# Attention features and two norms moved to ScalarE, the attention norm's scale and bias folded into the projections, and a new order of work in a three-stage pipeline

## The chip, the cores and the metric

The kernel runs on one core of a Trainium2 chip. The metric is the device time of one execution in microseconds (us), from launch to end. The profile is one execution recorded by the hardware profiler; its span is the time from the first to the last instruction. Five engines run side by side, each through its own queue in program order, and meet only at semaphores: TensorE (PE, with its weight loads PEld), VectorE (DVE), ScalarE (ACT), GpSimd (POOL) and SyncE (SP, which issues most DMAs).

## What is computed

Four layers, each a residual on a normed input, over `x` of 4 x 1024 x 256 float32. Cut to what matters:

```python
x = x + mamba(norm(x))          # projection, convolution, a scan over 1024 tokens, gate, projection, layer norm
x = x + ffn(norm(x))            # 8 experts 256 -> 256 -> 256, the two best weighted per token
x = x + attn_b(norm(x))
x = x + ffn(norm(x))            # the same weights as before

def attn_b(inputs):             # 16 heads of 16, causal linear attention
    x = layer_norm(inputs, ln1_scale, ln1_bias)
    q, k, v = x @ wq, x @ wk, x @ wv
    phi_q, phi_k = relu(q) + 0.001, relu(k) + 0.001
    num = phi_q . cumsum(phi_k v^T);  den = phi_q . cumsum(phi_k)
    x = (num / den) @ wo + inputs
    y = layer_norm(x, ln2_scale, ln2_bias)
    return x + gelu(y @ w1 + b1) @ w2 + b2
```

The scan is `s = clip(s * A + b_t x_t, -10, 10)` with a state of 256 x 32 per batch row, one token after another. It can't be reordered.

## The kernel before

`front_part` does the first projection, the convolution and the scan's operands for all tokens (some 95 us). `main_part` then goes over the 1024 tokens in 16 chunks of 64 tokens (4 batch rows x 64 = 256 rows, two tiles of 128). It is a pipeline of three stages that is written out by hand: `step(i, c, late)` scans chunk `i`, finishes the Mamba layer and runs the first expert layer and the attention of chunk `c = i - 1`, and runs the MLP's rest and the second expert layer of chunk `late = i - 2`. Step 1 has no `late`; then come 14 steps with all three stages (a hardware loop), then one without a scan and one with `late` alone. Each engine's function lists its operations in the order in which they go into its queue, so this list is the schedule.

- DVE: `scan(a, b)` makes scan steps a to b-1, each two multiplications (L1626) and two saturating additions (L1635), with ScalarE's `u(s)` (L928) as input, at most 8 ahead. Between them stand the norms' statistics (`ln_stats`), `add_expert` (L1748), `low_half`, `routing`, `mask`, `attended`, and, before the change, `ln_apply` for the outer norm (L1669), `ln_affine` for attention's norm (L1692, L1697), `key_feature` (L1820) and `query_feature` twice (L1826).
- PE: `y(n)` reads 8 finished scan steps (L1220). `first_layer` (L1287, three products of split operands, 12 matmuls) and `second_layer` (L1300, 4 matmuls) are an expert's two halves, `mlp_first` and `mlp_second` the MLP's. `tpose_set` transposes (L1234). The attention is `features` (L1375), `values` (L1382), `turn_k` (L1397), `scores` (L1408), `from_states` (L1418), `from_chunk` (L1428), `new_states` (L1439), `attention_out` (L1389).
- ACT: `relu` (L1035), `gelu` (L1055), `ln_apply` (L983), copies out of PSUM (`copy_set` L992, `copy_y` L1011, `copy_v`, `copy_k`), `spread_kv` (L1027).
- POOL: `rstd_of` makes a norm's factor in small steps (L821 to L828); `add_attention` (L879), `add_mlp_bias` (L872), `next_cblk` (L840).

PSUM has eight banks, and most are shared: `features` writes keys, then queries, into `HB[1]`, so the queries wait until `key_feature` has read the keys, and `TB` serves every transposition. `relu` of an expert stands between its `first_layer` and its `second_layer`, `add_expert` between one `second_layer` and the next on the same bank.

## Time and profile before

| | us |
|---|---|
| median of 3 runs | 1843.38 (1839.24 to 1846.09) |
| the profiled execution, its own time | 1845.13 |
| its span | 1843.3 |
| PE busy / DVE busy / ACT busy / POOL busy | 1693.8 / 1565.0 / 926.0 / 245.1 |
| from the start of step 1 to the start of step 2 | 104.8 |
| the 14 steps with all three stages | 1427.1, or 101.9 each |
| the two steps without a scan | 150.9 |

A step is counted here from one `gate_y` (L1760, four DVE instructions) to the next. Busy time is the union of an engine's instructions; an engine's idle time matters only where another waits for it.

### The profile page before, as it was taken

Reading aid. Unit: us, or ns where it says so; the run is one execution under the profiler, and the core shown is the slowest. Engines: PE = TensorE matmul, PEld = TensorE weight load, DVE = VectorE, ACT = ScalarE, POOL = GpSimd, SP = SyncE. Lnnn points to the kernel's source line nnn. Section 1 sums busy time; section 2 is a strip of 40 time slices with the busy share of each in tenths; the row PEclk is TensorE's granted clock in tenths of the full one; section 3 lists DMA queues with packets and bytes.
Section 4 is the critical chain, followed back from the end, with each engine's and each line's share of the span. In section 5 each row is a group of like instructions: output and inputs, shape, how many; then the busy total and the mean of one; then the engine's idle time right before and its main releaser. Section 6 shows DMA issues by size and latency. Waiting matters only on the chain. (4 is left out here: it accounts for less than half of the span.)

```text
span 1843.3 us, 55933 instructions
## 1 busy us (share of the span) xinstructions
PE 1693.8 (92%) x16992; PEld 1422.4 (77%) x16992; DVE 1565.0 (85%) x5957; ACT 926.0 (50%) x2134; POOL 245.1 (13%) x515
## 2 busy tenths in 40 slices
PE   5774889999999999999999999999999999999987
PEld 3332668787887878787888878787878878787986
DVE  6589879899998989898999999898989999997522
ACT  4674445463645555554645555455536455554322
POOL 1011011111102011110102020111101020111000
PEclk9886879999999989998999999899989999999998
DMA  6885333242333333332433323332423333330000
GB/s 191 298 247 147 110 94 99 77 117 75 102 96 90 100 84 110 91 96 77 110 87 93 107 81 98 100 99 81 117 71 93 105 89 104 93 98 20 1 7 6
DMA packets 108425, 182.63 MB, mean 99 GB/s; under 512 B 45288, under 2 KB 71936, under 8 KB 107648
## 3 DMA queue, kind: packets, MB, share of 16 engines
q1 hardware_dynamic: 107232, 178.71, 33.9%
q8 instruction: 146, 2.39, 0.6%
q14 instruction: 119, 0.97, 0.2%
q10 hardware_dynamic: 928, 0.56, 0.1%
HBM read 161.35 MB, written 17.83 MB: 97 GB/s over the span
## 5 line engine op out<-in xcount | busy, mean ns | idle before, releaser
L1635 DVE CUSTOM_DVE_ANT_0 state<-decayed_state,u_ring 128x128 f32<-128x128 f32 x2048 | 522.3, 293 | 11.1 <-ACT u_ring L928 4.7
L1626 DVE TENSOR_TENSOR decayed_state<-state,decay 128x128 f32<-128x128 f32 x2048 | 508.1, 289 | 2.7 <-POOL m_rstd L813 1.2
L1300 PE MATMUL bank<-f_w_sb,hs_whole 128*128 128x256 f32 x2048 | 488.3, 382 | 0.6 <-DVE res L1748 0.6
L928 ACT ACTIVATE u_ring<-xrep,b_steps 128x256 f32<-128x256 f32 x1024 | 450.5, 503 | 52.5 <-DVE state L1635 46.0
L1300 PEld LDWEIGHTS bank<-f_w_sb,hs_whole 128*128 128x128 f32 x2048 | 374.2, 191 | 45.9 <-DVE res L1748 1.0
L1035 ACT ACTIVATE hs_whole<-bank,f_b_sb 128x256 f32<-128x256 f32 x512 | 214.1, 470 | 373.1 <-PE bank L1287 373.1
L1287 PE MATMUL bank<-late_fT_parts,f_w_hi 128*128 128x256 f32 x1024 | 187.6, 306 | 0.0
L1287 PE MATMUL bank<-fT_parts,f_w_hi 128*128 128x256 f32 x1024 | 179.5, 297 | 4.6 <-DVE fT_parts L1678 3.4
L1220 PE MATMUL bank<-state,cblk 128*32 128x256 f32 x2048 | 151.3, 423 | 16.4 <-DVE state L1635 16.4
L1287 PEld LDWEIGHTS bank<-fT_parts,f_w_hi 128*128 128x128 f32 x1024 | 142.5, 189 | 23.3 <-DVE fT_parts L1678 7.1
L1287 PEld LDWEIGHTS bank<-late_fT_parts,f_w_hi 128*128 128x128 f32 x1024 | 149.8, 194 | 11.8 <-issue 5.8
L1748 DVE SCALAR_TENSOR_TENSOR x<-bank,comb,x 128x256 f32<-128x256 f32 x256 | 111.6, 478 | 19.5 <-PE bank L1300 19.4
L1748 DVE SCALAR_TENSOR_TENSOR res<-bank,comb,res 128x256 f32<-128x256 f32 x256 | 111.7, 478 | 15.5 <-PE bank L1300 11.7
L1300 PE MATMUL bank<-m_w_sb,hs_whole 128*128 128x256 f32 x512 | 118.3, 379 | 0.0
L1220 PEld LDWEIGHTS bank<-state,cblk 128*32 128x32 f32 x2048 | 59.2, 117 | 75.4 <-issue 36.3
L1300 PEld LDWEIGHTS bank<-m_w_sb,hs_whole 128*128 128x128 f32 x512 | 94.9, 190 | 11.6
L879 POOL TENSOR_TENSOR mb<-mb,a_t 128x512 f32<-128x512 f32 x16 | 20.5, 1279 | 608.2 <-DVE a_t L1813 608.2
L992 ACT ACTIVATE turn<-bank 128x512 f32<-128x512 f32 x48 | 28.6, 595 | 136.5 <-PE bank L1234 136.5
L821 POOL TENSOR_TENSOR m_ve<-m_mv,m_eps 128x2 f32<-128x2 f32 x96 | 20.7, 216 | 562.7 <-DVE m_mv L1662 562.7
L1287 PE MATMUL bank<-late_fT_parts,m_w_hi 128*128 128x256 f32 x512 | 91.4, 301 | 0.0
L1287 PE MATMUL bank<-late_fT_parts,f_w_lo 128*128 128x256 f32 x512 | 83.1, 286 | 0.0
L1287 PE MATMUL bank<-fT_parts,f_w_lo 128*128 128x256 f32 x512 | 81.0, 281 | 0.0
(157 smaller groups left out, 2296.3 us busy)
## 6 DMA issues: line engine op xcount, KB each, us to landing
xrep<-xs_dram SPq DMA_DIRECT2D x1024, 128.0 KB, 2.6
xt<-in_x SPq DMA_DIRECT2D x4, 1024.0 KB, 7.7
xn_dram<-xn SPq DMA_DIRECT2D x4, 1024.0 KB, 5.6
xs_dram<-xs SPq DMA_DIRECT2D x8, 512.0 KB, 4.4
f_w_sb<-in_f_w SPq DMA_DIRECT2D x2, 2048.0 KB
z_dram<-zT SPq DMA_DIRECT2D x8, 512.0 KB, 4.5
z_t<-z_dram SPq DMA_DIRECT2D x64, 64.0 KB, 2.3
out<-x SPq DMA_DIRECT2D x64, 64.0 KB, 2.1
```

What stands on the lines that cost most here:

```text
L821: pool.tensor_tensor(ve[:, k], mv[:, k, :, 1], eps[:, k], ALU.add).then_inc(ve_done[k].sem, 1)
L879: pool.tensor_tensor(mb[:], mb[:], a_t[:], ALU.add).then_inc(mb_done.sem, 1)
L928: act.activation(u_ring[:, s % USLOTS], xrep[:, slot, n], ACT.Copy, scale=b_steps[:, s // BSTEPS, s % BSTEPS:s % BSTEPS + 1]).then_inc(u_m ...
L992: act.activation(whole[:].rearrange("p k q -> p (k q)"), (HB[1] if k == T_WO else TB)[:], ACT.Copy).then_inc(tcopied[k].sem, 1)
L1035: act.activation(hs_whole[:, e % 2, m], hidden_bank(c, f, e)[:, m * TOK:(m + 1) * TOK], ACT.Relu, bias=g["f_b1"][:, e, m:m + 1]).then_inc( ...
L1220: last = pe.matmul(Y[YCOLS * j:YCOLS * (j + 1), tile * D:(tile + 1) * D], cblk[:, slot * YCOLS:(slot + 1) * YCOLS], state[:, s % RING, :], ...
L1287: last = pe.matmul(dst(tile), *((w_, d_) if stationary == "w" else (d_, w_)), start=first and stationary != "more", stop=(n == len(PRODUCT ...
L1300: last = pe.matmul(bank_[:, tile * D:(tile + 1) * D], hs_whole[:, slot, m, tile * P:(tile + 1) * P], w(m), start=(m == 0 and tile == 0 and ...
L1626: dve.tensor_tensor(decayed_state[:, part], state[:, (s - 1) % RING, part], decay[:, part], ALU.mult).then_inc(decayed.sem, 1)
L1635: dve._custom_dve(add_sat, out=state[:, s % RING, part], in0=decayed_state[:, part], in1=u_ring[:, s % USLOTS, part], s0=LIMIT, s1=-LIMIT) ...
L1748: dve.scalar_tensor_tensor(out=dst[:, tile], in0=out_bank(c, f, e)[:, tile * D:(tile + 1) * D], scalar=comb[:, f, tile, e:e + 1], in1=dst[ ...
```

## The change

1. The outer norm of attention's input moves from DVE (`ln_apply`, two instructions) to ScalarE (two `ln_apply` instructions, with a shift that POOL makes).
2. Attention's norm loses its scale and bias: ScalarE multiplies `wq`, `wk`, `wv` by `ln1_scale` once, in chunk 0, and PE makes the biases once. In the chunks ScalarE writes (x - mean) * rstd in two instructions, where DVE had four. The bias is added where the projections are read: in the features, and for the values in the copy before `attention_out` (two instructions for one).
3. The features move to ScalarE: `relu(x + bias)` per group of 128 rows, then `+ 0.001` over both groups; three instructions for one of DVE, three times per chunk.
4. POOL makes two small products more for each of the two norms. `add_attention` goes to the end of its queue.
5. The lists of all four engines are written in a new order.

```diff
+            def projections_scale(k):
+                act.wait_ge(mlp_bias_made.sem, 1)
+                for w in ("wq", "wk", "wv"):
+                    act.activation(g[w][:, k, :], g[w][:, k, :], ACT.Copy, scale=g["ln1_s"][:, k:k + 1]).then_inc(proj_scaled.sem, 1)
...
+                if k == T_WO:
+                    act.wait_ge(proj_bias_set.sem, 3)
+                    for kk in range(KD):
+                        act.activation(turn[:, kk], HB[1][:, kk * TOK:(kk + 1) * TOK], ACT.Identity,
+                                       bias=proj_bias[:, WV, kk:kk + 1]).then_inc(tcopied[k].sem, 1)
+                    return
...
+            def key_feature(c):
+                if c is None:
+                    return
+                act.wait_ge(proj_bias_set.sem, 3)
+                act.wait_ge(k_made.sem, k_made.after(c, 1))
+                for gr in range(KGROUPS):
+                    act.activation(kT[:, gr], HB[1][:, gr * TOK:(gr + 1) * TOK], ACT.Relu, bias=proj_bias[:, WK, gr:gr + 1]).then_inc(k_raw.sem, 1)
+                act.wait_ge(k_raw.sem, k_raw.after(c, KGROUPS))
+                act.activation(kT[:].rearrange("p k q -> p (k q)"), kT[:].rearrange("p k q -> p (k q)"), ACT.Identity,
+                               bias=g["feature_eps"][:, PADH // DH:PADH // DH + 1]).then_inc(kT_done.sem, 1)
+
+            def query_feature(c, half):
...
+                    act.activation(qT[:, KGROUPS * half + gr], HB[1][:, gr * TOK:(gr + 1) * TOK], ACT.Relu,
+                                   bias=q_bias[:, half, gr:gr + 1], scale=g["feature_own"][:, half:half + 1]).then_inc(q_raw.sem, 1)
```

Of ScalarE's list, from the outer norm to the scores:

```diff
+                ln_apply(c, OUTER, res, a_t, a_done)
                 u(33)
-                relu(late, 1, 0)
+                relu(late, 1, 2)
                 u(34)
                 u(35)
                 u(36)
+                ln_apply(c, LN1, a_t, turn, xl_done)
                 u(37)
...
                 u(43)
+                key_feature(c)
                 u(44)
+                u(45)
                 relu(late, 1, 4)
...
                 u(48)
+                query_feature(c, 0)
                 u(49)
+                copy_v(c)
+                query_feature(c, 1)
+                copy_k(c)
+                relu(late, 1, 5)
```

Of PE's list, the expert layers, then attention and the end of a step:

```diff
                 second_layer(c, 0, 3)
+                turn_comb(late, 1)
+                second_layer(c, 0, 4)
                 first_layer(c, 0, 5)
-                second_layer(c, 0, 4)
-                turn_comb(late, 1)
+                first_layer(c, 0, 6)
                 second_layer(c, 0, 5)
-                first_layer(c, 0, 6)
                 bias(late, 1)
+                second_layer(c, 0, 6)
                 first_layer(c, 0, 7)
...
                 features(g["wk"], k_made)
+                second_layer(late, 1, 3)
+                pe.wait_ge(kT_done.sem, kT_done.after(c, 1))
+                features(g["wq"], q_made)
+                values()
                 second_layer(late, 1, 4)
                 first_layer(late, 1, 5)
-                values()
-                pe.wait_ge(kT_done.sem, kT_done.after(c, 1))
-                features(g["wq"], q_made)
...
                 from_chunk(1).then_inc(num_made.sem, 1)
+                second_layer(late, 1, 6)
+                tpose_set(c, T_WO, at_done, HB[1])
+                y(5)
+                pe.wait_ge(tcopied[T_WO].sem, tcopied[T_WO].after(c, KD))
+                attention_out()
+                first_layer(late, 1, 7)
                 new_states(0).then_inc(kv_half.sem, 1)
                 wait_apart(kv_half, kv_half.after(c, 1))
                 new_states(1).then_inc(kv_made.sem, 1)
...
-                y(6)
+                second_layer(late, 1, 7)
                 pe.wait_ge(kv_added.sem, kv_added.after(c, 1))
                 tpose_set(c, T_MLP, yl_done)
-                second_layer(late, 1, 7)
-                y(OCTS - 1)
+                y(6)
...
                 mlp_first(c, 0)
+                y(OCTS - 1)
```

Of DVE's list, attention and the end of a step:

```diff
-                scan(43, 44)
-                query_feature(0)
-                query_feature(1)
-                scan(44, 46)
+                scan(47, 50)
                 mask(0)
...
-                scan(51, 57)
-                add_states()
-                scan(57, 59)
+                scan(55, 56)
+                add_expert(late, 1, 6, x3)
+                scan(56, 58)
                 add_attention()
                 ln_stats(c, LN2, a_t, xr_done, (1, 1))
-                scan(59, 61)
-                add_expert(late, 1, 6, x3)
-                scan(61, 64)
+                scan(58, 59)
+                add_states()
+                scan(59, 63)
                 low_half_mlp()
+                scan(63, 64)
                 add_expert(late, 1, 7, x3)
```

Where the order moves, three places matter. First PE in the hardware loop, behind `from_chunk`, before (L1439 is `new_states`, L1234 the transposition of the attended values, L1220 `y(5)`, L1389 `attention_out`, L1300 `second_layer`):

```order
L1428 MATMUL bank<-vv,ss 64x17 x64
L1439 MATMUL bank<-vv,ktok 32x17 x64
L1234 MATMUL bank<-ident_sb,turn 128x128 x4
L1214 REGISTER_ALU
L1215 REGISTER_ALU
L1220 MATMUL bank<-state,cblk 32x256 x8
L1389 MATMUL bank<-wo_sb,turn 128x256 x4
```

And of the changed kernel (L1488 was L1428, L1356 was L1300, L1499 was L1439):

```order
L1488 MATMUL bank<-vv,ss 64x17 x64
L1377 REGISTER_ALU
L1378 REGISTER_ALU
L1356 MATMUL bank<-f_w_sb,hs_whole 128x256 x4
L1290 MATMUL bank<-ident_sb,turn 128x128 x4
L1270 REGISTER_ALU
L1271 REGISTER_ALU
L1276 MATMUL bank<-state,cblk 32x256 x8
L1449 MATMUL bank<-wo_sb,turn 128x256 x4
L1343 MATMUL bank<-late_fT_parts,f_w_hi 128x256 x4
L1343 MATMUL bank<-late_fT_parts,f_w_lo 128x256 x4
```

The small matmuls of `new_states` no longer follow those of `from_chunk`: `second_layer(6)` stands there, and they come behind `attention_out` and `first_layer(7)`. The second place is PE at the loop's end, before (the last row transposes `y` for the next step):

```order
L1220 MATMUL bank<-state,cblk 32x256 x8
L1287 MATMUL bank<-late_fT_parts,m_w_hi 128x256 x4
L1287 MATMUL bank<-late_fT_parts,m_w_lo 128x256 x4
L1287 MATMUL bank<-late_fT_parts,m_w_hi 128x256 x4
L1579 REGISTER_ALU
L1579 COMPARE_AND_BRANCH
L1234 MATMUL bank<-ident_sb,turn 128x128 x4
```

And now:

```order
L1343 MATMUL bank<-late_fT_parts,m_w_hi 128x256 x4
L1343 MATMUL bank<-late_fT_parts,m_w_lo 128x256 x4
L1343 MATMUL bank<-late_fT_parts,m_w_hi 128x256 x4
L1270 REGISTER_ALU
L1271 REGISTER_ALU
L1276 MATMUL bank<-state,cblk 32x256 x8
L1641 REGISTER_ALU
L1641 COMPARE_AND_BRANCH
L1290 MATMUL bank<-ident_sb,turn 128x128 x4
```

`y(7)` and `mlp_first(c, 0)` have changed places, so that the transposition of `y` now follows `y(7)` directly. The third place is ScalarE ahead of the scores, in the changed kernel:

```order
L1031 ACTIVATE qT<-bank,q_bias,feature_own_sb 128x256 x2
L1033 ISA
L1035 ACTIVATE qT<-qT,feature_eps_sb 128x512
L935 REGISTER_ALU
L936 ACTIVATE u_ring<-xrep,b_steps 128x256
L1061 ACTIVATE vv<-bank 128x16x16 x2
L1031 ACTIVATE qT<-bank,q_bias,feature_own_sb 128x256 x2
L1033 REGISTER_ALU
L1035 ACTIVATE qT<-qT,feature_eps_sb 128x512
L1091 ACTIVATE ktok<-bank 128x512
```

Before, only the copies of the values and of the turned keys stood in this place on ScalarE, with scan inputs between them.

## Rows read from the trace of the kernel before

**Rows 1.** The page: span, busy time by engine, then its costliest group (us, mean ns).

```profile
span 1843.3 us, 55933 instructions
PE 1693.8 (92%) x16992; PEld 1422.4 (77%) x16992; DVE 1565.0 (85%) x5957; ACT 926.0 (50%) x2134; POOL 245.1 (13%) x515
...
L1635 DVE CUSTOM_DVE_ANT_0 state<-decayed_state,u_ring 128x128 f32<-128x128 f32 x2048 | 522.3, 293 | 11.1 <-ACT u_ring L928 4.7
```

**Rows 2.** Stretches: length, busy time per engine (instructions), granted clock, DMA, GB/s.

```profile
160.50:265.30 104.80, 74.45 (x794) 58.94 (x795) 89.81 (x338) 44.63 (x103) 14.49 (x27) 0.73 0.33 90
265.30:1692.40 1427.10, 1380.73 (x14506) 1188.47 (x14505) 1312.93 (x5097) 744.39 (x1778) 202.84 (x420) 0.96 0.33 93
...
1285.70:1390.70 105.00, 99.80 (x1039) 86.03 (x1038) 93.78 (x365) 53.14 (x128) 14.53 (x31) 0.95 0.33 92
1390.70:1491.10 100.40, 97.03 (x1038) 83.51 (x1037) 93.73 (x365) 53.26 (x128) 14.50 (x31) 0.98 0.35 96
```

**Rows 3.** Who waited for whom: total us, times, longest; PE, then ACT.

```profile
PE bank L1234 <- ACT late_turn L983: 32.8, 17, 4.5
PE bank L1408 <- issue: 9.3, 4, 2.7
PE bank L1408 <- DVE qT L1826: 5.1, 16, 1.2
...
ACT turn L1011 <- PE bank L1220: 22.3, 16, 8.0
```

**Rows 4.** PE in order of time, end of the last full step (start, us).

```profile
1668.94 4.51 PE L1428 MATMUL bank<-vv,ss 64*64 64x17 f32 x128
1673.39 1.05 PE L1439 MATMUL bank<-vv,ktok 64*32 64x17 f32 x64
...
1676.65 1.94 PE L1220 MATMUL bank<-state,cblk 128*32 128x256 f32 x16
...
1680.48 1.89 PE L1300 MATMUL bank<-f_w_sb,hs_whole 128*128 128x256 f32 x8
...
1683.71 1.07 PE L1220 MATMUL bank<-state,cblk 128*32 128x256 f32 x16
1686.93 0.63 PE L1234 MATMUL bank<-ident_sb,late_turn 128*128 128x128 f32 x4 [2.15 <-ACT late_turn L983]
```

**Rows 5.** The stretch of that step at the lower clock, columns as in rows 2.

```profile
1672.00:1680.00 8.00, 7.82 (x184) 5.94 (x181) 6.24 (x30) 2.99 (x7) 0.00 (x0) 0.57 0.01 3
```

**Rows 6.** DVE groups that go: count, busy us, mean ns, idle before.

```profile
L1669 DVE TENSOR_SCALAR a_t<-res,m_mv,m_rstd 128x256 f32<-128x256 f32 x32 | 25.0, 820 | 0.9 <-POOL m_rstd L825 0.9
L1826 DVE TENSOR_SCALAR qT<-bank,feature_floor_sb,feature_eps_sb 128x512 f32<-128x512 f32 x32 | 24.5, 806 | 25.4 <-PE bank L1375 25.4
L1692 DVE SCALAR_TENSOR_TENSOR turn<-a_t,m_mv,ln_s_sb 128x256 f32<-128x256 f32 x32 | 14.0, 478 | 0.0
L1820 DVE TENSOR_SCALAR kT<-bank 128x512 f32<-128x512 f32 x16 | 11.0, 685 | 2.2 <-PE bank L1375 2.2
```

**Rows 7.** ACT groups nearest to what comes, same columns.

```profile
L928 ACT ACTIVATE u_ring<-xrep,b_steps 128x256 f32<-128x256 f32 x1024 | 450.5, 503 | 52.5 <-DVE state L1635 46.0 <-DMA xrep<-xs_dram 6.3
L1035 ACT ACTIVATE hs_whole<-bank,f_b_sb 128x256 f32<-128x256 f32 x512 | 214.1, 470 | 373.1 <-PE bank L1287 373.1
L983 ACT ACTIVATE turn<-res,m_shift,m_rstd 128x256 f32<-128x256 f32 x32 | 17.5, 594 | 24.9 <-POOL m_shift L828 24.9
L358 ACT ACTIVATE xaT<-bank,in_b_sb 128x512 f32<-128x512 f32 x16 | 10.7, 684 | 9.7 <-PE bank L430 9.5
```

**Rows 8.** POOL in order of time, same step.

```profile
1682.71 1.29 POOL L879 TENSOR_TENSOR mb<-mb,a_t 128x512 f32<-128x512 f32 x1 [37.61 <-DVE a_t L1813]
1683.95 0.25 POOL L821 TENSOR_TENSOR m_ve<-m_mv,m_eps 128x2 f32<-128x2 f32 x1
```

**Rows 9.** ACT in order of time: the norm before the MLP, then `copy_y`.

```profile
1685.70 1.09 ACT L983 ACTIVATE late_turn<-a_t,m_shift,m_rstd 128x256 f32<-128x256 f32 x2 [1.04 <-POOL m_shift L828]
...
1690.36 0.60 ACT L1011 ACTIVATE turn<-bank 128x512 f32<-128x512 f32 x1 [0.84 <-PE bank L1220]
```

More of the change, by code:

```diff
@@ L1379, in values @@
                 def values():
+                    if late is None:
+                        pe.wait_ge(proj_scaled.sem, 3 * KD)
                     for tile in range(TILES):
@@ L1605, in mlp_bias_add @@
                                   ALU.add).then_inc(mlp_bias_set.sem, 1)
+                first = 2 * MLP // P
+                dve.tensor_copy(proj_bias[:].rearrange("p w m -> p (w m)"),
+                                TB[:, first:first + 6 * KD].rearrange("p (m u) -> p m u", u=2)[:, :, 0]).then_inc(proj_bias_set.sem, 1)
+                dve.wait_ge(proj_bias_set.sem, 1)
+                for half in range(PADH // DH):
+                    dve.tensor_scalar(q_bias[:, half], proj_bias[:, WQ], g["feature_own"][:, half:half + 1], None, ALU.mult).then_inc(proj_bias_set.sem, 1)
             def bias_low():
```

239 lines of the change are left out of this document (118 added, 121 removed).

## Prediction

> **What bounds the kernel now.** I read the page first: over the whole span PE is busy 92%, DVE 85%, ACT 50% [rows 1]. Busy shares mix stages, so I cut the span into steps next. The 14 full steps take 1427.1 of 1843.3 us, or 101.9 each, and there PE is busy 1380.7 us (97%) and DVE 1312.9 (92%) [rows 2]. So in most of the kernel PE is the bound, and DVE, with 93.8 us of work per step, is close behind. Only step 1 is different: PE is busy 74 of 104.8 us and DVE 90, at a mean clock of 0.73.
>
> The full steps are not alike: ten take 100.4 to 102.1 us and four 104.2 to 105.0; one of each kind stands in [rows 2]. PE's work is the same, its time is not. With the mean clock at 0.98, PE is busy 97.0 us; over all 14, at 0.96, it is 98.6. A mean of 0.98 over 100.4 us is some 4 us at 1.2 GHz instead of 2.4, 0.96 some 8. So 4 us more at the lower level cost PE 1.6 us, and at full clock throughout it would need about 95.5. I use this as the floor.
>
> Where the low clock falls is seen in [rows 4, 5]: after 4.5 us of `from_chunk` (17 columns each) and during `new_states`, 8 us have a mean of 0.57, so nearly 7 us of them are at the lower level. `y(5)` takes 1.94 us there, and 1.07 at full clock further down [rows 4]. The clock fell behind a row of small matmuls and rose again before the full-size ones had gone on for long.
>
> The rest over the floor is waiting. PE waits 17 times for the norm before the MLP, 32.8 us [rows 3]; three of them are in steps 1 and 16 and in the last one (up to 4.5 us), so I take 1.6 us for a full step. Sixteen times it waits for the query feature, 0.3 each. Four times it stands 2.3 us in the middle of the scores for "issue", that is for nothing that another engine does [rows 3]; those are the long steps (105.0 for 100.4, with a low stretch more).
>
> **What the change does to each engine.** DVE loses, per chunk, the outer norm (2 x 820 ns, 1.6 us), four instructions of attention's norm (4 x 478, 1.9; L1697 is as long as L1692), the keys (0.7) and the queries (1.6) [rows 6]: 5.8 us by mean durations, so 93.8 becomes 88. ScalarE gains two norms (4 x 594 ns, overlapping, 2.2 us), the keys' two `relu` (0.84 back to back, from 470 each) and an addition over 512 columns, the queries' four `relu` with a scale pointer as well (at most 594 each, 2.2) and two additions [rows 7]. The addition over 512 columns is not in the trace; `xaT`, 512 columns from PSUM with a pointer bias, takes 684 ns [rows 7], and two instructions of 256 columns at 594 bound it above at 1.2. I take 0.7, the nearest row. With 0.25 for the split copy this is 7.6 us, and 53 becomes 61 of 100. Neither engine is full. POOL's four small products (0.25 us each, [rows 8]) lie beside other work, and would cost 0.25 each if they stood on the chain.
>
> None of this is PE's. PE's 95.5 us stay, so DVE's 5.8 us count only where PE waited for DVE. I went through a step, with the durations of the rows, and looked at each wait of PE.
>
> 1. Norm before the MLP. Before, between `attention_out` and this transposition stood 3.2 us of experts (1680.48 to 1683.71, [rows 4]) and `y(6)`, 1.0; now `first_layer(7)`, `new_states` and `second_layer(7)`, 1.5 + 2.1 + 1.7 = 5.3 us. The chain is shorter too: `mb` (1.29 us) no longer stands ahead of POOL's first step [rows 8], 0.3 us, and DVE has no `add_states` ahead of `add_attention`. The wait goes: 1.6 us per step. What is late next is the low half of the MLP's operand. DVE reaches it behind four scan steps (0.9 us each: two additions of 293 ns [rows 1] and two multiplications as long, overlapping) and `add_states`, which waits for the now later `new_states`. By hand PE waits 0.6 for it and another 0.4 until scan step 64 is done for `y(7)`: +1.0, between 0.3 and 1.9 (two scan steps).
> 2. Scores. The queries' matmuls come one pair of expert layers earlier, and the chain on ScalarE is longer by about as much; the 0.3 goes. Cover: ScalarE ends `copy_k` only 0.3 us before PE needs it.
> 3. Keys. Between keys and queries PE now has only `second_layer(3)`, 1.7 us, before 4.9. `key_feature` takes 0.84 + 0.7 and two hand-overs of 0.1, 1.7. Taken as 0; if a `relu` stands ahead of it, 0.84.
> 4. `y(7)` last. Before, `mlp_first` hid `copy_y`; now `y` is transposed directly behind `y(7)`. PE pays the copy of 0.60 us [rows 9] and two hand-overs (the norm ends on ScalarE at 1686.79 and PE starts at 1686.93, 0.14 later [rows 4, 9]): +0.8, in every step.
> 5. `second_layer(c, 0, 6)` comes one expert layer earlier and needs `add_expert(4)`, which stands behind four scan steps: +0.4, between 0 and 0.9.
>
> Waits: -1.6 - 0.3 + 1.0 + 0.8 + 0.4 = +0.3 per step. The order itself gains nothing here.
>
> 6. The clock. `from_chunk` is now followed by `second_layer(6)`, and `new_states` stands between full-size layers. The row of small matmuls is 5.6 us (with `from_states`) instead of some 10. Before, the common step had nearly 7 us at the lower level, which cost 2.7, and the best one about half of it. I take half now, 1.3 us less. Bounds: nothing less, and all of it gone, 2.7. But the stretch that stays now falls on `second_layer(6)` and the matmuls behind it, which double (as `y` does in [rows 4]), while `from_chunk` hardly did. So I count 1.0.
>
> The Trainium skill, "TensorE: Matmul & The Clock Gate" ("HAM oscillation"), says that pauses of PE are what makes it fall back to the lower clock. By that alone nothing would be gained here, since PE is busy throughout; [rows 4, 5] speak against it, as PE is busy 7.8 of the 8 us there and yet at 0.57.
>
> 7. The stalls for issue. They come where PE runs through 128 records of the scores in 1.6 us; the scores stay where they are. I leave them: 0, between +4.6 us in each of the other ten steps and -4.6 in four.
>
> Full steps: (0.3 - 1.0) x 14 = -10 us. Step 1 is bound by DVE and its hand-overs: it loses 5.8 us of DVE work and gains 1.0 of `y(7)`; some of the time is spent waiting for PE at 1.2 GHz, so -3.5, between 0 and -5.8. The steps without scan: the norm's wait of 2.0 goes, ScalarE's longer chains give back 1: -1. Chunk 0: six scaled copies of 256 columns (503 ns, [rows 7]), 3 us on ScalarE, which is ahead and waits 8.0 us at the end of that chunk [rows 3]; without that cover 3 us. With four small DVE instructions: +0.5.
>
> Sum: -10 - 3.5 - 1 + 0.5 = -14. The profiled execution has 1845.1 us (2 us over its span, 1.7 over the median of 1843.4). -14 makes 1831 for it, and 1830 beside the median. A measurement of this kernel can tell 0.5%, 9 us, from no change.
>
> **The rivals.**
> - *The stalls go as well.* ScalarE's scan inputs no longer come in a bunch of five right behind `copy_k`, and each group of four makes SP load 512 KB just when PE streams the scores. For: the stall hits only four steps of 14, so it is a collision. Against: nothing names what PE waits for. Four times 4.6 less is 1812; the low clock gone altogether, 1.7 x 14 = 24, is 1806. Chance 0.17. (The Trainium skill, "Runtime: NRT & Kernel Launch", "Instruction fetch mechanics", holds that instructions are fetched ahead and hidden; by that the wait would not be there at all, and [rows 3] show it.)
> - *Hidden anyway.* PE is the bound, and its low stretches stay as they are: (0.3 x 14) - 4 = 0, 1843. For: PE's work is the same. Chance 0.22.
> - *The low stretch moves onto full-size matmuls: slower.* If the clock stays low for the same 6.8 us, it now falls on `second_layer(6)`, `y(5)` and `attention_out`, which all take twice as long: 3.4 us instead of 2.7. Then (0.3 + 0.7) x 14 - 4 = +10, 1853, and 1858 with the upper bounds of 1. It decides as soon as the low stretch is no shorter than before. For: the small matmuls before it alone last 5.6 us. Chance 0.10.
> - *ScalarE's chain is late.* `relu` and scan inputs stand ahead of the features and `HB[1]` is held longer: 0.84 us at the keys and 0.3 at the scores, 1.1 x 14 = 16: 1846. Against: ScalarE has 39 us left per step. Chance 0.09. The Trainium skill, "ScalarE: Activation LUTs" ("Rules for kernel authors"), advises VectorE for `relu` and additions; by durations the rows agree (one DVE instruction of 0.69 against three of together 1.5), and this rival is what that rule would do here.
> - That the change does not do what it says is excluded by the order of instructions, but for the values' bias, which costs the same either way.
>
> **How the numbers follow.** The forecast, 1830 with 1820 to 1841 around it, has 0.42. Faster by over 0.5% is below 1834: 0.34 of the forecast's, 0.17 of the first rival, 0.02: 0.53. Slower is above 1853: 0.01 of the forecast, 0.03 hidden, 0.06 and 0.04 of the last two with their upper bounds, 0.02 for mishaps: 0.16. Within it 0.31. The range, 1804 to 1856, takes in all cases but the tails of the second and fourth.
>
> **What the profile would show.** Right: a full step of 101.2 on average; no PE idle time before the transposition of `late_turn`; 0.8 before that of `y`, ended by ScalarE's copy; DVE busy 88, ACT 61 per step; half as long a low stretch per step, in `from_chunk` or behind it. Wrong: PE waiting for `kT` or `qT`; low stretches of the same length; stalls in the scores gone or more frequent; DVE's wait for POOL or ScalarE around the outer norm.

## The result: slower by 2.5%, and the profile after

The changed kernel takes 1889.0 us (median of 4 runs, 1886.4 to 1892.5), the kernel before 1843.7 beside it: ratio 1.025, 95% interval 1.0223 to 1.0277. Forecast were 1830 us and a range of 1804 to 1856, so the time lies 33 us above the range, and the change went the other way. The profiled execution is the longest of the four, 1892.5 us with a span of 1890.4.

The page of the changed kernel, its span and its busy time by engine, then the group that answers to the last of [rows 1]:

```profile
span 1890.4 us, 56208 instructions
PE 1729.9 (92%) x17016; PEld 1450.0 (77%) x17016; DVE 1519.6 (80%) x5816; ACT 1032.9 (55%) x2364; POOL 260.2 (14%) x579
...
L1703 DVE CUSTOM_DVE_ANT_0 state<-decayed_state,u_ring 128x128 f32<-128x128 f32 x2048 | 552.5, 307 | 54.7 <-PE bank L1276 26.2 <-ACT u_ring L936 20.0 <-issue 7.6
```

The stretches that answer to [rows 2] (step 1, the 14 full steps, the last full step; columns as there):

```profile
166.40:273.70 107.30, 74.91 (x796) 58.67 (x796) 86.88 (x329) 50.21 (x115) 14.65 (x31) 0.75 0.32 87
273.70:1739.20 1465.50, 1410.03 (x14505) 1210.15 (x14504) 1275.08 (x4970) 836.29 (x1974) 216.95 (x476) 0.95 0.32 91
1635.00:1739.20 104.20, 100.36 (x1038) 86.27 (x1037) 91.08 (x355) 59.16 (x140) 15.58 (x34) 0.95 0.26 73
```

Chunk 0 up to the first `gate_y` is 5.9 us longer (166.4 for 160.5), step 1 by 2.5, the 14 full steps by 38.4 (104.7 each for 101.9), the steps without scan by nothing. So the loss is in the full steps. Of their 38.4 us PE is busy for 29.3 more (1410.0 for 1380.7), with the same matmuls, and idle for 9.1 more. DVE is at 91.1 us per step where 88 were forecast, though over the whole kernel it has 141 instructions fewer (5816 for 5957). And one group that the change does not touch has become slower: the scan's second instruction, 2048 of them, has a mean of 307 ns where it had 293 [rows 1].

PE's waits, as in [rows 3]:

```profile
PE bank L1343 <- DVE late_fT_parts L1745: 32.0, 14, 2.3
...
PE bank L1290 <- ACT turn L1054: 12.4, 16, 0.8
PE bank L1290 <- ACT late_turn L998: 7.8, 2, 4.5
...
PE bank L1310 <- ACT fT_parts L1048: 5.0, 15, 1.3
PE bank L1356 <- DVE res L1809: 4.3, 14, 0.3
```

The wait for the norm before the MLP (17 times before) is left in two places outside the full steps. The wait for `copy_y` is there, 0.8 us, and that for `add_expert`, 0.3, both as forecast. There is no stall for issue in the scores of any full step. New is a wait of 2.3 us in each of the 14 full steps, for the low half of the MLP's operand (L1745), where 0.6 was forecast. What DVE does ahead of it, in order of time at the end of the last full step (start, us; x2 is two instructions that overlap):

```profile
1728.34 0.53 DVE L1694 TENSOR_TENSOR decayed_state<-state,decay 128x128 f32<-128x128 f32 x2
1728.80 1.60 DVE L1703 CUSTOM_DVE_ANT_0 state<-decayed_state,u_ring 128x128 f32<-128x128 f32 x2
1730.33 0.57 DVE L1694 TENSOR_TENSOR decayed_state<-state,decay 128x128 f32<-128x128 f32 x2
1730.82 0.51 DVE L1703 CUSTOM_DVE_ANT_0 state<-decayed_state,u_ring 128x128 f32<-128x128 f32 x2
1731.24 0.49 DVE L1694 TENSOR_TENSOR decayed_state<-state,decay 128x128 f32<-128x128 f32 x2
1731.65 1.60 DVE L1703 CUSTOM_DVE_ANT_0 state<-decayed_state,u_ring 128x128 f32<-128x128 f32 x2
...
1734.00 0.68 DVE L1745 TENSOR_TENSOR late_fT_parts<-bank,late_fT_parts 128x512 fp32r<-128x512 f32 x1
```

And POOL in the same stretch:

```profile
1728.69 1.32 POOL L880 TENSOR_TENSOR mb<-res,mlp_b_sb 128x512 f32<-128x512 f32 x1
...
1731.79 1.31 POOL L887 TENSOR_TENSOR mb<-mb,a_t 128x512 f32<-128x512 f32 x1
```

A pair of scan instructions takes 0.51 us, but twice 1.60, and each time POOL is in one of its two additions of 128x512. One of the pair is held until the addition ends, 1.36 us for 0.29, so the two cost DVE 2.1 us. I call this a hold. The trace books it as busy time, not as a wait. Over the kernel 28 of the 2048 scan additions take over 1.3 us, two in each full step; before, the longest took 0.34. The change moved the additions here: `add_mlp_bias` stood behind the first of POOL's last three reciprocal roots, `add_attention` ahead of the last one, and now both stand behind all of them, beside the scan's last steps and just ahead of what PE waits for.

PE at the same place, in order of time (compare [rows 4]):

```profile
1718.12 3.39 PE L1356 MATMUL bank<-f_w_sb,hs_whole 128*128 128x256 f32 x8
...
1727.78 1.99 PE L1356 MATMUL bank<-f_w_sb,hs_whole 128*128 128x256 f32 x8
...
1731.76 0.63 PE L1343 MATMUL bank<-late_fT_parts,m_w_lo 128*128 128x256 f32 x4
1734.74 1.23 PE L1343 MATMUL bank<-late_fT_parts,m_w_hi 128*128 128x256 f32 x4 [2.34 <-DVE late_fT_parts L1745]
1735.89 1.94 PE L1276 MATMUL bank<-state,cblk 128*32 128x256 f32 x16
1738.55 0.66 PE L1290 MATMUL bank<-ident_sb,turn 128*128 128x128 f32 x4 [0.72 <-ACT turn L1054]
```

After the wait of 2.34 us the clock is at its lower level: `mlp_first`'s last four take 1.23 us for 0.63, `y(7)` 1.94 for 1.07. By the granted clock there is a second low stretch (a time at 1.2 GHz instead of 2.4) here in all 14 full steps of this execution, beginning 99 to 103 us into the step, beside the one near 81 us, which now lies on `second_layer(6)` (3.39 us for 1.99). Together they are 11.5 us per step; before, they were 7.6.

### The profile page after: what moved, and what is told of

The parts are those of the page before. It is cut to its first block and busy times, and to the rows that moved or that the text cites. A ratio compares the mean times of both kernels' runs of the same rounds, so it can differ in the third digit from the quotient of the medians.

```text
span 1890.4 us, 56208 instructions
## 1 busy us (share of the span) xinstructions
PE 1729.9 (92%) x17016; PEld 1450.0 (77%) x17016; DVE 1519.6 (80%) x5816; ACT 1032.9 (55%) x2364; POOL 260.2 (14%) x579
## 5 line engine op out<-in xcount | busy, mean ns | idle before, releaser
L1703 DVE CUSTOM_DVE_ANT_0 state<-decayed_state,u_ring 128x128 f32<-128x128 f32 x2048 | 552.5, 307 | 54.7 <-PE bank L1276 26.2
L1356 PE MATMUL bank<-f_w_sb,hs_whole 128*128 128x256 f32 x2048 | 509.4, 395 | 6.0 <-DVE res L1809 4.3
L1694 DVE TENSOR_TENSOR decayed_state<-state,decay 128x128 f32<-128x128 f32 x2048 | 508.3, 289 | 2.7 <-POOL m_rstd L821 1.2
L1356 PEld LDWEIGHTS bank<-f_w_sb,hs_whole 128*128 128x128 f32 x2048 | 388.8, 198 | 58.4 <-issue 9.3
L1343 PE MATMUL bank<-late_fT_parts,f_w_hi 128*128 128x256 f32 x1024 | 176.0, 297 | 2.0 <-issue 2.0
L1343 PE MATMUL bank<-fT_parts,f_w_hi 128*128 128x256 f32 x1024 | 170.3, 294 | 0.0
L1343 PEld LDWEIGHTS bank<-late_fT_parts,f_w_hi 128*128 128x128 f32 x1024 | 142.9, 190 | 11.5 <-issue 7.9
L1343 PEld LDWEIGHTS bank<-fT_parts,f_w_hi 128*128 128x128 f32 x1024 | 141.2, 192 | 7.8 <-issue 6.2
L1098 ACT ACTIVATE hs_whole<-bank,m_b_sb 128x256 f32<-128x256 f32 x128 | 53.6, 470 | 147.1 <-PE bank L1343 147.0
L1343 PE MATMUL bank<-late_fT_parts,m_w_hi 128*128 128x256 f32 x512 | 97.7, 324 | 32.8 <-DVE late_fT_parts L1745 32.0
L1356 PE MATMUL bank<-m_w_sb,hs_whole 128*128 128x256 f32 x512 | 115.9, 379 | 0.0
L1343 PEld LDWEIGHTS bank<-late_fT_parts,m_w_hi 128*128 128x128 f32 x512 | 80.0, 216 | 43.3 <-DVE late_fT_parts L1745 34.9
L1356 PEld LDWEIGHTS bank<-m_w_sb,hs_whole 128*128 128x128 f32 x512 | 96.0, 190 | 12.3
L1010 ACT ACTIVATE turn<-bank,proj_bias 128x256 f32<-128x256 f32 x32 | 13.4, 471 | 138.5 <-PE bank L1290 138.5
L1343 PE MATMUL bank<-fT_parts,f_w_lo 128*128 128x256 f32 x512 | 81.6, 282 | 0.0
```

The source lines that it names most:

```text
L1010: act.activation(turn[:, kk], HB[1][:, kk * TOK:(kk + 1) * TOK], ACT.Identity, bias=proj_bias[:, WV, kk:kk + 1]).then_inc(tcopied[k].sem, 1)
L1098: act.activation(hs_whole[:, j % 2, m], HB[j % 2][:, m * TOK:(m + 1) * TOK], ACT.Gelu_apprx_tanh, bias=g["m_b1"][:, 2 * j + m:2 * j + m + ...
L1343: last = pe.matmul(dst(tile), *((w_, d_) if stationary == "w" else (d_, w_)), start=first and stationary != "more", stop=(n == len(PRODUCT ...
L1356: last = pe.matmul(bank_[:, tile * D:(tile + 1) * D], hs_whole[:, slot, m, tile * P:(tile + 1) * P], w(m), start=(m == 0 and tile == 0 and ...
L1694: dve.tensor_tensor(decayed_state[:, part], state[:, (s - 1) % RING, part], decay[:, part], ALU.mult).then_inc(decayed.sem, 1)
L1703: dve._custom_dve(add_sat, out=state[:, s % RING, part], in0=decayed_state[:, part], in1=u_ring[:, s % USLOTS, part], s0=LIMIT, s1=-LIMIT) ...
```

## Experiments

Theory 1: POOL's additions hold the scan, PE waits for the low half, and with the exposed `copy_y` this opens the second low stretch; and the products for the folded bias cost chunk 0 some 5 us. Rival 2: ScalarE's new work costs the time. Rival 3: only where the low stretch falls matters. In the diffs "-" is the changed kernel and "+" the experiment. Ratios are to the kernel before, run beside it on the same chip.

**POOL's additions in their old places** (`e1`)

```diff
                 rstd_of(c, OUTER)
+                add_mlp_bias()
                 next_cblk(1)
                 rstd_of(c, LN1)
                 next_cblk(2)
+                add_attention()
                 rstd_of(c, LN2)
                 next_cblk(3)
-                add_mlp_bias()
...
                 next_cblk(7)
-                add_attention()
```

> The changed kernel with one part undone: GpSimd's two 128x512 additions stand again where they stood before the change (add_mlp_bias behind the first reciprocal root, add_attention behind the second). Theory 1 (each of them, beside the scan, holds one VectorE instruction L1703 for 1.36 us instead of 0.29, +2.1 us on VectorE's way to low_half_mlp, and the TensorE waits this makes let its clock fall a second time): the longest L1703 falls to under 0.6 us, TensorE's wait ahead of L1343 from 2.3 us to 0.2 to 0.8, the second stretch at 1.2 GHz at the step's end gets shorter; a full step 104.7 -> 100.5 to 103, total 1832 to 1866 us. Rival 2 (the features and the attention norm on ScalarE cost the time): the wait at L1343 stays above 1.5 us and the total stays within 5 us of 1889. Rival 3 (only where the low clock falls matters): the wait goes, the low stretches stay as long, total 1857 to 1870 us.

Measured: 1815.7 us (1809.8 to 1821.3), ratio 0.985 (0.9797 to 0.9903). This one edit takes the ratio from 1.025 to 0.985. The 14 full steps and the last one:

```profile
269.40:1656.30 1386.90, 1360.66 (x14505) 1172.94 (x14504) 1255.08 (x4971) 835.03 (x1974) 214.40 (x476) 0.99 0.34 96
1558.50:1656.30 97.80, 95.99 (x1037) 82.96 (x1036) 89.65 (x356) 59.51 (x141) 15.31 (x34) 1.00 0.29 78
```

DVE and PE ahead of and behind the low half:

```profile
1651.81 0.51 DVE L1703 CUSTOM_DVE_ANT_0 state<-decayed_state,u_ring 128x128 f32<-128x128 f32 x2
1652.24 0.68 DVE L1745 TENSOR_TENSOR late_fT_parts<-bank,late_fT_parts 128x512 fp32r<-128x512 f32 x1
```

```profile
1652.98 0.74 PE L1343 MATMUL bank<-late_fT_parts,m_w_hi 128*128 128x256 f32 x4
1653.81 1.07 PE L1276 MATMUL bank<-state,cblk 128*32 128x256 f32 x16
1655.60 0.66 PE L1290 MATMUL bank<-ident_sb,turn 128*128 128x128 f32 x4 [0.72 <-ACT turn L1054]
```

No scan instruction is held at the end of a step, PE's wait at L1343 is gone, and no step has a low stretch at its end (six have none at all). The holds themselves are not all gone. Some 50 us into each full step `add_mlp_bias` makes one scan multiplication take 0.73 us for 0.28, and at 88 to 91 us `add_attention` makes another take up to 0.59; PE waits for neither. The first of them in the last full step:

```profile
1608.53 1.28 POOL L880 TENSOR_TENSOR mb<-res,mlp_b_sb 128x512 f32<-128x512 f32 x1
```

```profile
1608.44 0.88 DVE L1809 SCALAR_TENSOR_TENSOR x<-bank,comb,x 128x256 f32<-128x256 f32 x2
1609.24 0.97 DVE L1694 TENSOR_TENSOR decayed_state<-state,decay 128x128 f32<-128x128 f32 x2
```

So what the old places take away is the hold just ahead of the low half. Against the changed kernel's profile the full steps lose 78.6 us: 49.4 of PE's busy time, which is the clock, and 29.2 of its idle time, which is the wait. Per step that is 3.5 and 2.1. Rivals 2 and 3 fall. The measured 1816 lies below the 1832 that theory 1 allowed: I had counted the wait and part of the second stretch, and it went whole.

**The old end of the step** (`e2`), with POOL as in the changed kernel: `y(7)` ahead of `mlp_first(c, 0)`, scan 63 ahead of the low half, `copy_y` ahead of `gelu`.

```diff
                 y(6)
+                y(OCTS - 1)
...
                 mlp_first(c, 0)
-                y(OCTS - 1)
...
-                scan(59, 63)
+                scan(59, 64)
                 low_half_mlp()
-                scan(63, 64)
...
-                gelu(c, 0)
                 copy_y(i)
+                gelu(c, 0)
```

> The changed kernel with another part undone: the end of the step as before (y(7) ahead of mlp_first(c, 0) on TensorE, scan 63 ahead of low_half_mlp on VectorE, copy_y ahead of gelu(c, 0) on ScalarE). Theory 1: TensorE's wait of 0.8 us for copy_y ahead of L1290 goes, the wait of 2.3 us ahead of L1343 stays (about 2.3 to 2.9 us, since low_half_mlp comes one scan instruction later), the second low-clock stretch stays in most steps: a full step 104.7 -> 103.5 to 104.7, total 1872 to 1889 us. Rival (the late y(7) and the exposed copy_y alone open the second low-clock stretch): it is gone, a full step 100.5 to 102.5, total 1832 to 1860 us.

Measured: 1875.1 us, ratio 1.0167 (1.0115 to 1.022), a full step 103.5. The copy is hidden and the rest of the wait has moved to `y(7)`, 3.6 to 3.7 us in each full step in place of 2.3 and 0.8:

```profile
PE bank L1276 <- DVE state L1703: 68.9, 21, 6.3
```

The scan is held as before (28 times), and a low stretch at the step's end is there in all 14. So the new end is not what brings it: with the wait of 3.7 us it comes in the old end as well.

**The folded bias's products spread** (`e3`): 4 of the 24 products behind each of six later gates, instead of all between the first gates of chunk 0.

```diff
-                        if n == 2:
-                            projections_bias()
                         if 2 <= n < 2 + MLP // P:
                             mlp_bias(n - 2)
+                        elif 2 + MLP // P <= n < 2 + MLP // P + 3 * KD:
+                            projections_bias(n - 2 - MLP // P)
...
-                    scan(0, 24)
+                    scan(0, 36)
                     mlp_bias_add()
```

> The changed kernel with TensorE's 24 products of the folded bias (L1245) no longer in one piece between the first gates of chunk 0, but four at a time behind six later gates, and VectorE's addition of the bias later in its scan. Theory 1: chunk 0 gets back most of the 5.4 us that this piece took, the full steps stay at 104.7: total 1883 to 1886 us. Rival (chunk 0's loss of 5.9 us comes from the scaling of the weights on ScalarE or from loads issued late): total 1888 to 1890 us, the first gate_y still at 166 us.

Measured: 1883.1 us, ratio 1.0201 (1.0147 to 1.0255), which overlaps that of the changed kernel; the first `gate_y` at 163.2 us. By the number theory 1 is met; the second profile of the changed kernel (`e13`, below) shows that this proves nothing.

**All three undone** (`e4`)

> The edits of the three kernels before this one together (GpSimd's additions in their old places, the old end of the step, the folded bias's products spread): what is left of the change is the features, the outer norm and the attention norm on ScalarE, the fold, the keys and queries there, and the new order of scores, states and second_layer. Theory 1: no wait over 0.5 us a step ahead of L1343 and L1290, one low-clock stretch in a step as in the kernel before, a full step 99.5 to 101.5, total 1808 to 1838 us, that is the same as the kernel before or up to 2% faster. Rival 2 (what moved to ScalarE costs the time): a full step above 103, total above 1860 us. Rival 3 (the low stretch on full-size matmuls of second_layer costs it): no waits, but a full step 101.5 to 103, total 1838 to 1860 us.

Measured: 1822.4 us, ratio 0.9869 (0.9817 to 0.9921), a full step 100.1. Once the scan is not held just ahead of the low half, the new end takes a little less: `e8` below differs from this run in the end alone and has 99.6 us per full step, and `e1`, also with the new end, 99.1. As times they can't be told apart. While the scan was held, the same end cost 1.2 (104.7 against 103.5 in `e2`).

**The old order of the states as well** (`e5`): on top of `e4`, `new_states` behind `from_chunk`, `second_layer(6)` behind `attention_out`, `add_states` early. What is left is ScalarE's new work, the fold, the new place of the keys and queries, and the new order of the expert layers ahead of the scores.

```diff
                 from_chunk(1).then_inc(num_made.sem, 1)
-                second_layer(late, 1, 6)
+                new_states(0).then_inc(kv_half.sem, 1)
+                wait_apart(kv_half, kv_half.after(c, 1))
+                new_states(1).then_inc(kv_made.sem, 1)
```

> The kernel with three edits undone, and also the states and second_layer in their old order (new_states right behind from_chunk, second_layer(6) behind attention_out, VectorE's add_states early again). What is left of the change is what moved to ScalarE, the fold, and the keys and queries. Theory 1 (ScalarE's new work is hidden and VectorE is free of 3.4 us a step): a full step 98 to 102 us, total 1812 to 1845 us, the low-clock stretch on new_states instead of second_layer. Rival 2 (what moved to ScalarE costs the time): above 1855 us, with waits of TensorE for L1010, L1013 or L998. Rival (the new order of states is where the gain lies): total at or above 1843 us, as the kernel before.

Measured: 1835.9 us (10 runs), ratio 0.9948 (0.9918 to 0.9977). The 14 full steps, and the new wait for `relu`:

```profile
267.40:1680.00 1412.60, 1373.16 (x14505) 1177.45 (x14504) 1253.17 (x4970) 832.98 (x1976) 213.66 (x476) 0.97 0.33 94
```

```profile
PE bank L1356 <- ACT hs_whole L1078: 15.1, 16, 1.0
```

A full step takes 100.9 us. So what moved to ScalarE, with its fold, is hidden. But it is not shown to be worth anything by itself: none of these steps has a stall for issue, and in the first profile of the kernel before the ten full steps without one average 100.8 us; all 14 have 101.9. The 0.5% is no more than the missing stalls give. The later place of `new_states` (`e4`) is worth another 0.8 us per step, by one profile each: with it that wait of 0.93 is gone, and the low clock is 3.9 us per step for 5.4.

**The additions cut to 2 columns** (`e6`): in their new places with their waits and signals, but from chunk 1 on 2 columns long. This leaves the MLP's bias and the attention out of the sum for the other columns.

```diff
-                    pool.tensor_tensor(mb[:], mb[:], a_t[:], ALU.add).then_inc(mb_done.sem, 1)
+                    if late is None:
+                        pool.tensor_tensor(mb[:], mb[:], a_t[:], ALU.add).then_inc(mb_done.sem, 1)
+                    else:
+                        pool.tensor_tensor(mb[:, 0, 0:2], mb[:, 0, 0:2], a_t[:, 0, 0:2], ALU.add).then_inc(mb_done.sem, 1)
```

> The changed kernel with GpSimd's two additions in their new places, waits and signals, but from chunk 1 on 2 of their 512 columns long (the MLP's bias and the attention are left out of the sum for the other columns). Theory 1 (an addition holds one VectorE instruction for as long as it runs itself): each addition takes under 0.4 us, no L1703 above 0.7 us, the wait ahead of L1343 is 0.2 to 0.6 us, a full step within 1 us of that with the additions in their old places (98.9), total 1808 to 1825 us. Rival 4 (the place in GpSimd's order, its waits and the later reciprocal root cost the time, not the length): the total stays above 1850 us.

Measured: 1816.8 us, ratio 0.982 (0.9765 to 0.9875). POOL, the two additions of the last full step:

```profile
1657.85 0.29 POOL L883 TENSOR_TENSOR mb<-res,mlp_b_sb 128x2 f32<-128x2 f32 x1
...
1661.16 0.24 POOL L893 TENSOR_TENSOR mb<-mb,a_t 128x2 f32<-128x2 f32 x1
```

The longest scan addition of the kernel takes 0.38 us, PE waits at most 0.2 us at the low half where it waited 2.3, a full step is 99.6. This decides between length and place: with the same place and the same waits, the time goes with the length of the additions. DVE is busy 88.9 us per step, 0.8 less than in `e1`.

**The kernel before with its additions late** (`e7`), here "-" is the kernel before:

```diff
                 rstd_of(c, OUTER)
-                add_mlp_bias()
                 next_cblk(3)
                 rstd_of(c, LN1)
                 next_cblk(4)
-                add_attention()
                 rstd_of(c, LN2)
+                add_mlp_bias()
                 next_cblk(5)
                 next_cblk(6)
                 next_cblk(7)
+                add_attention()
```

> The kernel before with one edit: its two GpSimd additions moved behind the last reciprocal root of the step (add_mlp_bias ahead of the last three next_cblk, add_attention behind them), beside the scan's last instructions. Theory 1: one or two scan instructions (L1635) of 1.3 us in each full step where there were none above 0.35 us, low_half_mlp 1.1 to 2.1 us later, a full step 101.9 -> 103.5 to 107, total 1865 to 1910 us. Rival (the blocking costs time only in the changed order): total 1838 to 1850 us.

Measured: 1860.5 us (10 runs), ratio 1.0042 (1.0003 to 1.008): slower, but hardly clear of the noise and by less than I had expected; neither of the two ranges was met. A full step takes 103.0 us. DVE and POOL at the end of a full step:

```profile
565.12 0.87 DVE L1748 SCALAR_TENSOR_TENSOR x<-bank,comb,x 128x256 f32<-128x256 f32 x2
565.91 0.97 DVE L1626 TENSOR_TENSOR decayed_state<-state,decay 128x128 f32<-128x128 f32 x2
566.80 0.57 DVE L1635 CUSTOM_DVE_ANT_0 state<-decayed_state,u_ring 128x128 f32<-128x128 f32 x2
567.29 1.55 DVE L1626 TENSOR_TENSOR decayed_state<-state,decay 128x128 f32<-128x128 f32 x2
```

```profile
565.22 1.27 POOL L872 TENSOR_TENSOR mb<-res,mlp_b_sb 128x512 f32<-128x512 f32 x1
...
567.18 1.31 POOL L879 TENSOR_TENSOR mb<-mb,a_t 128x512 f32<-128x512 f32 x1
```

The second addition holds a scan instruction in the same way, here the multiplication (L1626). The first one began beside `add_expert` (L1748), which has an operand in PSUM and took its usual 0.87 us for two; only the multiplication behind it was held, for 0.4 us. The shortest full step went from 100.4 to 101.2 us. So the hold comes in the old order too, and what it costs depends on what DVE has in hand when it begins.

This run also says something of the clock. PE now waits twice at the end of a full step, for the norm and for `y(7)`:

```profile
PE bank L1220 <- DVE state L1635: 37.4, 23, 6.3
PE bank L1234 <- ACT late_turn L983: 31.6, 17, 4.5
```

Together that is 1.9 to 3.6 us at a step's end, and 3.0 or more in six of the 14, as much as the 3.0 to 3.1 of the changed kernel. Yet no step has a low stretch there.

**One addition back** (`e10`): only `add_mlp_bias` in its old place, so that one hold is left instead of two.

> The changed kernel with only add_mlp_bias back in its old place; add_attention stays at the end of GpSimd's step, so one scan instruction a step is held for 1.36 us instead of two. If the wait is all that counts and the clock follows it, half of the loss is left: L1703 above 0.7 us 14 times instead of 28, the wait ahead of L1343 1.1 to 1.4 us (it was 2.3 with two, none with none), a full step 100.5 to 103 (98.9 with none, 104.7 with two), total 1838 to 1865 us. Rival A (the second low-clock stretch opens only beyond some length of wait): a full step under 100.3, total 1822 to 1836 us. Rival B (any wait at that place opens it): a full step above 103, total above 1865 us.

Measured: 1822.8 us (10 runs), ratio 0.9947 (0.9926 to 0.9968), a full step 100.1. It is not the half of the hold that I meant. `add_attention` now begins just ahead of the low half:

```profile
1664.28 1.34 POOL L887 TENSOR_TENSOR mb<-mb,a_t 128x512 f32<-128x512 f32 x1
```

```profile
1664.39 0.68 DVE L1745 TENSOR_TENSOR late_fT_parts<-bank,late_fT_parts 128x512 fp32r<-128x512 f32 x1
1664.99 0.97 DVE L1694 TENSOR_TENSOR decayed_state<-state,decay 128x128 f32<-128x128 f32 x2
```

L1745 reads a bank of PSUM and is not held; the multiplication behind it is, for the last 0.5 us. PE waits 0.6 us for `y(7)` instead of 2.3 for the low half, and there is no low stretch at the step's end. Both numbers of rival A are met. But `e7`, with waits as long as the changed kernel's and no such stretch, does not fit a rule by the length of the wait alone.

**Code moved, and both kernels once more** (`e11`, `e12`, `e13`)

> The kernel before with 64 empty instructions ahead of TensorE's main part, so that its instructions lie elsewhere in memory; nothing else. In the kernel before 4 of 14 full steps stand still for 1.9 to 2.7 us in the scores (L1408) with no wait that the profile shows; the changed kernel and all its variants have none of these. If they come from where the code lies: another number or other steps (fewer than 3 or more than 6 of them, or at another line), total 1830 to 1850 us. If they come from what the steps do (VectorE's and ScalarE's work beside the scores): again 4 or 5 stalls at L1408 in every second or third step, total within the runs of the kernel before.

> The kernel before, unchanged, for a second profile. In the first, TensorE stood still for 1.9 to 2.7 us in the scores (L1408) in 4 of 14 full steps; with its instructions moved by 64 places in 2 of 14. If the place of the code decides: the same steps as in the first profile. If it varies between executions: other steps or another number, span 1830 to 1850 us.

> The changed kernel, unchanged, for a second profile. In the first, the low clock lasted from 89.4 to 116.7 us and the first gate_y came at 166.4 us; kernels with the same chunk 0 code had it at 162.2 to 163.7 us. If chunk 0's loss of 5.9 us belongs to the change: again 165 to 168 us. If it is one execution's clock: 161 to 164 us. Scan instructions held above 1.3 us: again two in each full step, the full step 104 to 105.5 us.

Measured: `e11` 1836.8 us, ratio 0.9999 (0.9974 to 1.0025), with stalls of 2.2 and 2.7 us in two full steps (5 and 14). The second profile of the kernel before (span 1843.2) has five, of 1.9 to 2.5 us, in full steps 1, 2, 4, 8 and 14, where the first had four, in 4, 6, 9 and 11. So they vary between executions, and `e11` says nothing of where code lies. But in the four profiles in the old order of everything (`e7` is the fourth, with five) there are 16 in 56 full steps, and in the ten of the changed kernel and its variants none in 140. What causes them and what ended them stays open.

The second profile of the changed kernel has a span of 1878.3 us, 27 held scan additions (in one full step it is a multiplication that is held in place of one), full steps of 104.1, and the first `gate_y` at 161.2 us, as the kernel before (160.5 and 162.0). The 5.9 us of chunk 0 thus belonged to one execution, whose low stretch there lasted 27 us, and not to the folded bias. That part of theory 1 falls. Its first full step had no low stretch at all:

```profile
268.50:368.40 99.90, 95.81 (x1038) 82.88 (x1037) 91.07 (x355) 59.58 (x142) 15.43 (x34) 1.00 0.33 95
```

Beside `e1`'s step at the same clock, 97.8 us, this measures the held scan by itself: 2.1 us per step (2.2 beside the steps of `e6` at that clock). The clock costs the changed kernel another 4.2 to 4.8 us in the mean step (104.1 and 104.7), and `e1` only 1.3 (99.1).

**Additions back and bias spread** (`e8`)

> The changed kernel with GpSimd's additions in their old places and the folded bias's products spread, the new end of the step kept. Theory 1: the two add up, first gate_y 1 to 3 us earlier than with the additions alone, full steps as there (98.9): total 1808 to 1818 us, faster than the kernel before by 1.3 to 2%. Rival (chunk 0 differs between executions by the clock alone): no earlier first gate_y, total within 3 us of 1816.

Measured: 1815.3 us, ratio 0.9834 (0.978 to 0.9887), the first `gate_y` at 159.4 us, a full step 99.6. Chunk 0 is 2.8 us earlier than in `e1`, no more than profiles of one kernel differ there, and the total is the same: spreading the bias brings nothing that can be told. Both beat the kernel before by about 1.6% and the changed kernel by about 4%.

## Why the prediction was wrong

**The step that failed** is step 1 of the hand walk: it has the path of DVE to the low half, and so PE's wait for it, wrong. I wrote that `mb` no longer stands ahead of POOL's first step and booked it as a gain of 0.3 us. I never asked what stands beside `mb` in its new place. "Between 0.3 and 1.9" for the low half and `y(7)` was bounded by DVE's order of instructions alone, each at its mean duration. Measured: two holds keep DVE 2.1 us from the low half, and PE waits 2.3. With the additions back in their old places (`e1`) it waits for nothing there, and with additions of 2 columns in the new places (`e6`) at most 0.2. The hint was in rows I had read: the outer norm's instruction took 820 ns at 256 columns, L1692 only 478 at as many [rows 6]. Here the mean hid two populations, and the line of the kernel before shows it (shortest, median, longest, ns):

```profile
L1669 DVE TENSOR_SCALAR a_t<-res,m_mv,m_rstd x32: 400/810/1372, 214.8 to 1741.2; 128x256 f32<-128x256 f32 x32
```

Sixteen of the 32 took 0.40 us and sixteen 1.22 to 1.37, and each of the latter ran beside `add_mlp_bias`, which held it. The Trainium skill has the rule, in "SBUF — State Buffer", section "Who interferes with whom": VectorE instructions with two inputs in SBUF contend with a GpSimd instruction that reads SBUF, for ports that the two engines share under an exclusive lock. The traces agree: L1703, L1694 and L1626 were held up to 1.36 us by additions of 1.31, those with an operand in PSUM (0.68 and 0.48 each) and the statistics, with one input (0.42), were not. L1669 has one such input; the section names `tensor_scalar` among the operations that can take the shared pair when their operands meet its conditions. It was the page to look up for a move of POOL's work.

**The clock** (step 6) had its sign wrong in the changed kernel, for the same reason. Forecast was 1.0 us less per step; PE's busy time rose by 2.1 (98.6 to 100.7). Without the holds ahead of the low half it fell by 1.4 (to 97.2 in `e1`). Some 0.5 of that belongs to the four steps with stalls, as the ten others had 98.1 before; the 0.9 that is left is near the 1.0 that I forecast from shorter rows of small matmuls. What I left out is that the wait could bring a new low stretch. By size this is most of the miss: a full step took 104.7 us for 101.2, and 3.1 of these 3.5 are PE's busy time (2.1 more where 1.0 less was forecast); the waits are 0.3 over the forecast, because the missing stalls (0.7) took back part of the low half's 1.3. With 2.3 and 0.8 us or with 3.7 us of waiting at the step's end (both profiles of the changed kernel, `e3`, `e2`), 55 of 56 full steps had a low stretch there; with 0.8, with 1.3 or with 0.6 and 0.8 (`e1`, `e4`, `e10`), none of 42 had. The Trainium skill's rule that pauses of PE bring the lower clock ("TensorE: Matmul & The Clock Gate", "HAM oscillation") I had weighed only as an objection. These rows agree with it; `e7` (1.9 to 3.6 us in two waits, none of 14) and the stretches near 81 us, which come with PE busy, are not told by the length of the waits alone. That the low stretch goes with the hold is shown by `e1` and `e6`; what exactly opens it stays open.

**The other terms** held. Step 1's norm wait went (1.6 forecast, none left). Steps 2 and 3: no wait for `kT` or `qT`. Step 4: 0.8 forecast, 0.8 measured. Step 5: 0.4 and 0.3. In `e1` the low half and `y(7)` wait for nothing, where +1.0 was forecast. Missing was a wait of 0.27 at the first gate (L1310). ScalarE was forecast at 61 us per step and is at 59.7; DVE at 88, and is at 91.1, or 88.9 with the additions cut. Of the 5.8 us that I took off DVE, 0.8 was the hold on the norm and no work of the norm.

**Step 7** was wrong: the stalls for issue are gone, 9.3 us in the full steps of the first profile. The four long steps averaged 104.7 us and the ten others 100.8, so the stalls with what follows them are worth some 15 us, by my estimate from these steps. This is the premise of my first rival (1806 to 1812), and the kernel with the additions in their old places lands near it, at 1816. Its 14 full steps have PE 20 us less busy and 20 us less idle than before [rows 2]; forecast were 14 less busy and 4 more idle.

**Step 1 of the kernel** (-3.5 forecast) takes 106 to 110 us in all ten profiles of the changed kernel and its variants, for 104.8 to 105.8 in the four profiles in the old order: some 2 more, although DVE has 3 to 4 us less to do. PE's largest pause there, before a transposition that waits for ScalarE, is 12.1 us for 12.7. So DVE's work may not have been what bounds it; no run took this apart.

**The rivals.** The slower side was forecast by the low stretch moving onto full-size matmuls, 1853 to 1858 at 0.10. It did move (3.39 us for 1.99 on `second_layer(6)`), but `e5` (100.9 us per full step) and `e4` (100.1) speak for a small gain by the new order. The case that came true, work of POOL that holds DVE just ahead of what PE waits for, was in none of them.

## What to carry to other kernels

An edit on a GpSimd queue has a second address: what VectorE executes while the moved instruction runs. Put a long elementwise GpSimd instruction beside VectorE work that reads PSUM or beside the statistics, never beside a chain of two-input instructions (or one like L1669) that somebody waits for, and look at shortest and longest durations of a group before its mean is used in a sum. And when a change adds a pause on TensorE, count the matmuls behind it at the lower clock as well: here 2.1 us of held scan cost 4.5 to 5.6 per step.

## What the runs showed of the hardware that I had not expected

- A GpSimd addition of 1.3 us held a VectorE instruction with two SBUF inputs that began beside it until the addition ended, the custom scan instruction (0.29 to 1.36 us) as well as a plain multiplication (0.28 to 1.36, and to 0.73 or 0.77 where the addition was already half done). The trace shows the hold as busy time of the held instruction.
- Waits of 3.0 to 3.2 us at the end of a step came with a low stretch in all steps but one of the changed kernel's two profiles and of `e3`, and in none of the six steps of `e7` with waits of 3.0 to 3.6.
- The same work in the same order differed between two executions by 12 us of span (1890.4 and 1878.3), 5 of them in where the low clock fell in chunk 0.
- Stalls of 1.9 to 2.7 us that no engine explains came in 16 of 56 full steps of the kernel before and its variants and in none of 140 of the changed kernel and its variants; their cause stays open.
